# Three routing scatters per half instead of two, near the end of the second attention

## The reference

```python
x = x + tanh(g_xattn[1]) * attention_1(ctx, layernorm(x), ctx, mask, ...)     # the "second attention"
x = x + tanh(g_ffn[1])   * experts(layernorm(x), router_w, router_b, w1, w2, w3)

def experts(x, ...):                       # E = 8 experts, K = 2 choices, cap = 1024
    scores = x_flat @ router_w + router_b
    top_scores, assign = top_k(scores, 2)
    gates = softmax(top_scores)
    pos = cumsum(cumsum(one_hot(assign), axis=0), axis=1)   # a token's place in its expert's list
    grouped = tokens collected by (expert, pos) where pos < cap
    h = gelu((grouped @ w2) * (grouped @ w1))
    eo = h @ w3
    out = eo[e_id, p_id] where the token had a place, else x
    return sum over the two choices of out * gates
```

## Time and profile before

| | us |
|---|---|
| three runs | 1035.28, 1035.51, 1038.65 (median 1035.51) |
| the profiled execution's own time | 1037.14 |
| its span, first to last instruction | 1035.3 |
| busy: PE, DVE, ACT, POOL | 909.9, 841.2, 677.7, 578.2 |
| mean granted TensorE clock | 0.954 of full speed |

### The profile page before, as it was taken

One profiled execution on the slowest core, in us unless ns is written; L12 is line 12 of the kernel. 1 busy time (PEld: TensorE's weight loads), 2 busy tenths in 40 slices (PEclk: granted clock), 3 DMA queues, 4 the chain that ended last, 5 costly groups with the idle time before them and its releaser, 6 DMA issues. The chain is left out here.

```text
span 1035.3 us, 30109 instructions
## 1 busy us (share of the span) xinstructions
PE 909.9 (88%) x11572; PEld 696.4 (67%) x11593; DVE 841.2 (81%) x2240; ACT 677.7 (65%) x1740; POOL 578.2 (56%) x736
## 2 busy tenths in 40 slices
PE   8999999999999980599958999997888999968775
PEld 5888879988888860276637888874446777733332
DVE  5999987878899984366648999987997999978987
ACT  5888874357777740154536777786876788856663
POOL 6444402343347767423158888714665478768884
PEclk9999999999999985799989999998999999969998
DMA  8670000000000001356311111000000000000000
GB/s 223 159 288 2 3 2 2 2 2 2 3 10 28 31 32 51 100 174 188 115 47 32 31 30 30 25 3 1 2 2 1 3 2 3 3 1 16 21 22 26
DMA packets 60527, 44.44 MB, mean 43 GB/s; under 512 B 15196, under 2 KB 55781, under 8 KB 59366
## 3 DMA queue, kind: packets, MB, share of 16 engines
q1 hardware_dynamic: 55718, 34.09, 11.1%
q0 software_dynamic: 4096, 8.34, 2.7%
q10 hardware_dynamic: 576, 0.13, 0.1%
HBM read 23.73 MB, written 18.87 MB: 41 GB/s over the span
## 5 line engine op out<-in xcount | busy, mean ns | idle before, releaser
L2111 DVE TENSOR_REDUCE rowmax<-ps 128x16 f32<-128x1024 f32 x128 | 155.4, 1214 | 27.2 <-PE ps L729 26.5
L1136 ACT ACTIVATE pr<-ps 128x512 f32<-128x512 f32 x256 | 139.0, 595 | 48.9 <-PE ps L798 45.5
L2117 DVE TENSOR_TENSOR sm<-ps,rowmax 128x512 f32<-128x512 f32 x256 | 164.9, 686 | 3.4
L798 PE MATMUL ps<-cst,sm 128*128 128x128 f32 x1024 | 142.0, 278 | 13.3 <-DVE sm L2117 9.6
L756 PE MATMUL ps<-vbd,pr 128*64 128x18 f32 x4096 | 141.7, 212 | 0.6 <-ACT pr L1136 0.5
L756 PEld LDWEIGHTS ps<-vbd,pr 128*64 128x64 f32 x4096 | 134.0, 138 | 5.2 <-ACT pr L1136 1.6
L798 PEld LDWEIGHTS ps<-cst,sm 128*128 128x128 f32 x1024 | 111.5, 141 | 32.5 <-issue 21.9
L1526 POOL TENSOR_SCALAR xn<-x_sb,mv_all,rstd_all 128x128 f32<-128x128 f32 x122 | 99.3, 814 | 35.8 <-PE ps L693 28.5
L1016 ACT ACTIVATE qbd<-ps,bqp,cst 128x128 f32<-128x128 f32 x256 | 104.8, 464 | 6.5 <-PE ps L709 2.7
L1313 POOL DMA_INDIRECT big<-expert_out,row_g x64 | 68.4, 1069 | 45.4 <-DMA expert_out<-xn_all 23.0
L1330 POOL DMA_INDIRECT slots<-xn_all,row_s x64 | 65.1, 1017 | 30.6 <-DVE sm L2117 15.9
(11 more groups left out here) (322 smaller groups left out, 2334.0 us busy)
## 6 DMA issues: line engine op xcount, KB each, us to landing
slots<-hT SPq DMA_DIRECT2D x8, 1024.0 KB, 10.7
sm<-slots SPq DMA_DIRECT2D x32, 256.0 KB, 3.2
expert_out<-xn_all SPq DMA_DIRECT2D x16, 256.0 KB, 2.9
ew<-in_L_ffn_w SPq DMA_DIRECT2D x24, 128.0 KB, 2.5
out<-x_sb SPq DMA_DIRECT2D x32, 64.0 KB, 1.5
slots<-xn_all,row_s POOLq DMA_INDIRECT x64
big<-expert_out,row_g POOLq DMA_INDIRECT x64
x_sb<-in_x SPq DMA_DIRECT2D x1, 512.0 KB, 4.5
```

The costliest lines, as they stand in the source:

```text
L798: last = nc.tensor.transpose(turned[b][:, r * P:(r + 1) * P], sm[x][:, c:c + P], ident)
L1136: nc.scalar.activation(pr[y][:, b, :], turned[b], ACT.Exp, scale=SCALE).then_inc(p_ready[y], 1)
L2111: v.tensor_reduce(row3, sc, AX.X, ALU.max).then_inc(rowmax_ready[x], 1)
L2117: v.tensor_tensor(sm[x][:, :].rearrange("p (r g k) -> p r g k", r=RG, k=S)[:, part], sc[:, part], row3[:, part].unsqueeze(3).broadcast_to( ...
```

## The change

In the last six halves of attention(1), t = 29 to 34, GpSimd issues three scatters instead of two. Their order among themselves is the same; scatters are now numbered n = 2 * tile + choice. The first stands at the head of the half as before. In these six halves the tile's deviation (`rstd`) stands directly behind this first scatter, and the second and third follow it (behind the same wait for the scores, where there is one). Halves 17 to 28 are as before: 24 scatters; the six last have 18; the loop behind attention(1) has 22 left. The number of scatters, their operands and every other engine's program stay the same.

```diff
-            def scatter(b, u, c, t=None):
+            def scatter(n, t=None):
+                u, c = divmod(n, 2)
+                b = next(b for b, (begin, end) in enumerate(BATCHES) if begin <= u < end)
...
-                u = t - (BATCHES[0][1] - 1 + ROUTE + 4)
-                if not 0 <= u < T or t >= T + 3:
-                    return None
-                return next(b for b, (first, end) in enumerate(BATCHES) if first <= u < end), u
+                first, by_three = BATCHES[0][1] - 1 + ROUTE + 4, T - 3
+                if not first <= t < T + 3:
+                    return []
+                begun = 2 * (min(t, by_three) - first) + 3 * max(t - by_three, 0)
+                return list(range(begun, begun + (2 if t < by_three else 3)))
...
-                    if l == 1 and scattered(t) is not None:
+                    sent_now = scattered(t) if l == 1 else []
+                    if sent_now:
                         if prev is not None:
                             pool.wait_ge(sm_ready[y], subtracted(l, prev))
-                        scatter(*scattered(t), 0, t)
+                        scatter(sent_now[0], t)
+                        if len(sent_now) > 2:
+                            rstd(k, oldest, y)
...
-                    if l == 1 and scattered(t) is not None:
+                    if sent_now:
                         if new is not None:
                             pool.wait_ge(s_psum[x], IT * l + new + 1)
-                        scatter(*scattered(t), 1, t)
+                        for n in sent_now[1:]:
+                            scatter(n, t)
...
-                    if oldest is not None and l == 1:
+                    if oldest is not None and l == 1 and len(sent_now) < 3:
                         rstd(k, oldest, y)
...
-                for u in range(max(first, scattered(T + 2)[1] + 1), end):
-                    for c in range(2):
-                        scatter(b, u, c)
+                for n in range(max(2 * first, scattered(T + 2)[-1] + 1), 2 * end):
+                    scatter(n)
```

## The result

The changed kernel took **1038.26 us** (median of 20 runs, 1036.95 to 1040.62), the kernel before 1036.16 beside it (20 runs, 1034.81 to 1038.83). The ratio is **1.0018, 95% interval 1.0011 to 1.0024**: slower by 0.2%, some 2 us, where 4.7 us less were forecast. The profiled execution has a span of 1037.0 us against 1035.3.

The account below looks back on a forecast made before the run. GpSimd's scatters, then the TensorE-bound expert loop, joined by one wait. Last scatter at 417.33 instead of 421.99, contention nothing: median 1035.51 less 4.66 gives 1030.9 us; range 1029.5 to 1034.0.

Parts of the forecast that it names:

- What bounds the kernel: Before the experts: GpSimd's scatters, then a TensorE-bound loop, joined by one 31.76 us wait; time off the scatters starts TensorE earlier.
- 0.90 us of idle time ahead of half 34's deviation: GpSimd in half 34: the wait before the deviation would be filled, as its statistics are done at 386.11, before 386.64.
- The sum of GpSimd's steps: Halves 29 to 34 and the loop behind: 4.38 us per half, 21 steps of 1.289, last scatter 4.66 us earlier.
- The third scatter fits: GpSimd in halves 30 and 29: the added scatter finishes before the next head's wait for VectorE ends, 0.13 us to spare.
- I take nothing: Contention of VectorE with the added scatters in six halves: zero cost assumed, from a 0.20 us operation at 390.08.
- My bounds for contention: VectorE beside the added scatters: from nothing up to a whole scatter, 0.97 us in each of six halves, 5.8 us.
- Rival D: Halves 29 to 34: VectorE is held by the third scatter; at one whole scatter per half 1036.6 us; chance 0.06.
- Rival C, the blends: Start of the experts: VectorE's leftover blends delay the first product, 1.1 to 2.5 us, most likely 1032.6; chance 0.15.
- pace that I cannot explain: VectorE's blends beside the scatters: 2.24 us each, where alone they take 0.47.
- The other covers: Target rows are written before scatters need them: 5.9 us ahead for batch 2 in half 31; batch 4 also ahead.
- The sign given for D: Profile after: growing distances of VectorE's row maxima in halves 29 to 31 would show VectorE held by the third scatter.

Follow-up runs that it names:

- r1: The changed kernel itself, run again in another job: 1025.13 us against 1029.85 for the kernel before, ratio 0.9963.
- r3: Kernel before with the deviation put between the two gathers of each half in attention(2): 1029.33 us against 1029.85, ratio 0.9997.
- r5: Kernel before with the deviation put between the two gathers of attention(2), in a job with a slower kernel before: 1029.94 us against 1036.61, ratio 0.9933.
- e4: Kernel before with both scatters of a half directly behind one another in halves 17 to 34: 1041.90 us against 1037.56, ratio 1.0043.
- e3: Changed kernel with the deviation between second and third scatter in halves 29 to 34: 1036.24 us against 1037.56 for the kernel before, ratio 0.9985.
- r6: Kernel before with a third scatter, set apart by the deviation, in halves 29 to 31, and attention(2)'s gathers spaced: 1029.20 us against 1036.61, ratio 0.9935.
- r4: Kernel before with both scatters directly behind one another in halves 17 to 34, in another job: 1028.84 us against 1029.85, ratio 0.9991.
- e1: Changed kernel's early deviation in halves 29 to 34, but two scatters per half and 28 behind: 1039.91 us against 1037.56 for the kernel before, ratio 1.0023.

## Why the prediction was wrong

**What bounds the kernel: right.** TensorE restarts 2.3 to 2.7 us behind the start of the last scatter in the kernel before, the changed kernel and r1 (2.70, 2.32, 2.70), and the medians of r1's own job differ by 4.7 us (interval 2.5 to 5.1). Its kernel before was not profiled there, but r3, which leaves attention(1) as it was, was: from the first scatter to the last it takes 118.52 us, r1 114.47, so the scatters end 4.05 us earlier like for like. The forecast had 4.66. Of the 0.90 us of idle time ahead of half 34's deviation, which it counts as filled, only 0.28 are there in r3 and in r5.

**The sum of GpSimd's steps: right, where nothing disturbs it.** By r1:

| | forecast | r1 | changed kernel |
|---|---|---|---|
| head of half 31 | 372.46 | 372.19 | 374.23 |
| head of half 34 | 385.66 | 385.40 | 391.61 |
| deviation of half 34 | 386.64 | 386.39 | 392.60 |
| last scatter | 417.33 | 416.85 | 422.99 |
| TensorE restarts | 420.0 | 419.55 | 425.31 |
| first product | 429.7 | 429.55 | 435.83 |

r1's own start was some 0.3 us early, and from there each mark keeps its distance within 0.3 us. The heads from half 32 to 34 are 4.37 and 4.38 apart (forecast 4.38), the 22 scatters behind are 21 steps of 1.290 (1.289).

**The steps that failed** are "The third scatter fits" in halves 30 and 29 and, under contention, "I take nothing". The third scatter fits into GpSimd's time, as r1 shows. It does not fit beside TensorE's value products in a job with the hold: three indirect DMAs with 0.30 to 0.53 us between them begin ahead of the products or beside them and end after them. The completion then comes 2.6 to 2.8 us late (halves 30, 31 and 33), VectorE's statistics with it, and the deviation, now queued ahead of two scatters, makes GpSimd wait 1.90 to 2.25 us. The early deviation thus turned a delay on TensorE into idle time on GpSimd: 6.14 us against a gain of 4.66, and 1.0 us net at the last scatter (6.14 less 4.66 less the 0.48 by which the undisturbed r1 lies ahead of the forecast). My bounds for contention took in only VectorE and GpSimd at SBUF. I had looked for slow operations, and this cost is in none: the operations of VectorE and GpSimd keep their length.

**Rival D** had the right sign and, by luck, nearly the size: one scatter of 0.97 us in each of six halves, 5.8 us, a time of 1036.6. But it named the wrong engine. In the changed kernel VectorE's routing operations with two SBUF inputs (lines 1842 and 1843) take 0.20 to 0.25 us beside scatters and 0.20 to 0.23 away from them. By the Trainium skill, "SBUF — State Buffer", section "Who interferes with whom", a VectorE instruction with two SBUF inputs contends with a GpSimd instruction that reads SBUF; at these operations the traces show no such cost. The normalisation (line 1831) takes 0.34 to 0.42 us beside scatters and 0.33 to 0.40 away from them. The chance of 0.06 was too small for a place where no row of three scatters beside value products existed.

**Rival C, the blends:** they did not take over. In the changed kernel they end at 433.40, and the product at 435.83 waits for ScalarE:

```profile
427.69 5.71 DVE L2175 SCALAR_TENSOR_TENSOR x_sb<-xn_all,wx,x_sb  x12 [0.17 <-issue]
435.83 0.69 DVE L2236 TENSOR_TENSOR pr<-ps,pr 128x512 f32<-128x512 f32 x1 [2.42 <-ACT pr L1205]
```

But the "pace that I cannot explain" was the clue that I had in hand. The same blends in r1:

```profile
397.28 0.63 DVE L2175 SCALAR_TENSOR_TENSOR x_sb<-xn_all,wx,x_sb  x2 [0.36 <-DVE wx L2165]
398.10 11.21 DVE L2175 SCALAR_TENSOR_TENSOR x_sb<-xn_all,wx,x_sb  x30 [0.18 <-issue]
429.55 0.69 DVE L2236 TENSOR_TENSOR pr<-ps,pr 128x512 f32<-128x512 f32 x1 [20.23 <-ACT pr L1205]
```

Thirty in 11.21 us, beside scatters that run back to back, where the earlier trace rows show 2.24 us for one. The scatters are the same in both. Over all 20 traces the two signs go together: in the nine with the hold the 32 blends last 28.8 to 37.3 us and attention(2) or attention(1) has lags over 0.9; in the eleven without it the blends last 12.0 to 12.1 us and the median lag is 0.02. That one cause is behind both signs is likely by this, not shown. So the earlier trace rows already showed the disturbance that the sum left out, and attention(2) of the kernel before, which I had not opened, showed it beside TensorE.

**The other covers: right.** GpSimd never stopped for rows in half 31: batch 2 is written at 371.33 in the changed kernel and its first scatter starts at 379.24. Batch 3, whose cover the prediction did not look at, had 4.2 us (394.17 + 0.16 to 398.55). The profile after has one scatter, a deviation, two scatters in each half, and 22 behind. The sign given for D, longer distances of the row maxima in halves 29 to 31, is what appeared, though by another cause: a sign of VectorE being late does not say who made it late.

**What stays open.** Shown: with the hold present, an indirect DMA that ends near the end of the value products or after it goes with a late completion (up to 0.97 us for one alone, 1.1 us for pairs in e4, up to 2.8 for three in the changed kernel, up to 4.0 for longer runs), and spacing removes most of it at an unchanged number (r5, and halves 30 and 31 of e3). The transfers themselves are not late: in the changed kernel and in r1 alike the first packets of half 29's scatters move 1.55 to 1.62 us behind the scatter's start. Not shown: what inside the chip is held, why it is there in some jobs and not in others (one chip had both), and whether the fixed part of a scatter or its 128 rows cause it. Not explained either are 12 of the 237 lags, whose report does not follow the end of a DMA within 0.75 us. That TensorE's matmuls themselves are late, and not only the report of their end, can't be told apart, as their ends in the trace are modelled.

**Which version to keep.** Spaced gathers alone: -0.67% with the hold, nothing lost without it (1.0000, 0.9997). Scatters as in the change: -0.37% without the hold, +0.18% with it. Both changes together gave -0.46% without it and weren't measured with it; r6, the more careful form, gave -0.65% with it.

## What to carry to other kernels

Before filling GpSimd's idle time with more indirect DMAs, look at what TensorE does in that place. Keep another operation between two of them, and place them so that the last ends before the dense small matmuls do (0.4 us before, here). Read the idle time ahead of a consumer ("remote", or a wait for an engine that was through by its record) and compare the semaphore event with the end of the producer; busy times alone hide these 6 us. If a row of the profile has a pace that nothing explains, find its cause before costing an edit that lies beside the same work, and measure the kernel in more than one job.

## What was not expected of the hardware

- In jobs with the hold, the completion of TensorE's 32 value products comes 2.60 us after their modelled end beside three indirect DMAs 0.30 and 0.53 us apart, and 1.07 to 1.23 us beside two. Beside a single one it is 0.02 where that one ends well ahead of the products and up to 0.97 where it does not.
- The same program has this in some jobs and not in others, and with it the kernel before takes 1036.2 to 1037.6 or 1028.4 to 1029.9 us (medians of six jobs). Attention(2), the same in before, r1 and r4, takes 143.9 us in the first and 135.1 in the other two.
- In the same jobs VectorE's blends, which take their addresses from registers, stand idle up to 3.15 us before one in the changed kernel and up to 4.55 in e1, beside GpSimd's scatters; in jobs without the hold 30 of them take 0.37 us each.
- An indirect DMA of 128 rows keeps GpSimd for 0.97 to 1.04 us, with 128 or with 64 columns, and for 0.90 us with 64 rows.
